# Bias product in pairs of 64 stationary columns, and the channels of a bank in runs of 32 and 96

## Chip, cores and metric

One Trainium2 chip, one core. The metric is the device time of one execution in microseconds (us); lower is better. Single instructions are given in nanoseconds (ns).

## What is computed

The input `x` is `(8, 32, 32, 384)`: 8 images of 32x32 pixels with 384 channels, in fp32. After a group norm (32 groups) the result is `x` plus the sum of two branches:

```python
def _L0_conv_ref(x, w1, b1, w2, b2, bias_w, bias_b):        # x is the normed input
    bias = x @ bias_w.T + bias_b                            # 384 x 384, every pixel
    xb = x.reshape(B, H, W, 4, 96)                          # 4 blocks of 96 channels
    xf = jnp.fft.rfftn(xb, axes=(1, 2), norm='ortho')
    xr, xi = (xf.real, xf.imag)
    r1 = relu(block_mul(xr, w1[0]) - block_mul(xi, w1[1]) + b1[0])
    i1 = relu(block_mul(xr, w1[1]) + block_mul(xi, w1[0]) + b1[1])
    r2 = block_mul(r1, w2[0]) - block_mul(i1, w2[1]) + b2[0]
    i2 = block_mul(r2, w2[1]) + block_mul(i1, w2[0]) + b2[1]
    out = jnp.fft.irfftn(complex(r2, i2), s=(H, W), axes=(1, 2), norm='ortho')
    return out.reshape(B, H, W, C) + bias
x = x + _L0_conv_ref(_gn(x), ...)
```

## The kernel before

The Fourier transforms are matmuls with tables. The work goes image by image (`image(b, p, ...)` on each engine: L703 for TensorE, L829 for ScalarE, L1007 for VectorE), and the order on each engine is written out by hand, with semaphores between them. The bias product is done on the frequency side: it is added to the second block product in the same PSUM bank, and the inverse transform along the width takes both back together.

The stages of one image on TensorE (`mm` at L520 issues every matmul, so all carry L521 in the profile):

- `c1` (L560): the first block product; units 0 to 7 use 128 stationary columns and 192 moving ones, unit 8 uses 32 stationary columns and 96 moving ones, 48 matmuls over the four quarters of a bank's partitions.
- `p3` (L599), with `p1` (L523) of the next image between: transforms along the height and, of the next image, along the width.
- `p4` (L622): the transform back along the height, 96 stationary columns and 128 moving ones; `c2_bias` of item 0 stands in its middle.
- the second block product with the bias, 8 items `gi` of 128 rows by 384 channels, each in a bank of its own (`g_bank`, L302). `c2_bias` (L657) opens the bank with 3 channel tiles `ct` of 3 matmuls each (`mm3`, L554: values are split into a high and a low fp16 part, and high x high, high x low and low x high are added). Its stationary operand is a strided column set of `y` (every 8th of 1024, two bytes each), 128 columns; 384 moving columns of `biasw`. `c2_rho` (L672) adds the block product: for each of 4 blocks, real and imaginary part and 3 products, two matmuls with 64 stationary columns and 96 moving ones, one into partitions 0 to 63 of the bank and one into 64 to 127: 24 pairs, 48 matmuls an item. Item 0 has one more matmul for each pair (`rhoX`), into partitions 64 to 127.
- `p6` (L691): the inverse transform along the width, 3 matmuls of 128 stationary and 384 moving columns for each of 8 tiles, the first three tiles ahead of `c2_rho` of item 7.

The order in the second product is: bias 1 and 2 after `p4`; rho 0, rho 1, `mean` of the next image, rho 2, bias 3, rho 3, `variance` of the next image, bias 4, rho 4, bias 5, rho 5, bias 6, rho 6, bias 7, `p6` tiles 0 to 2, rho 7, `p6` tiles 3 to 7, then `c1` of the next image. The last image has no `mean` and `variance`, and its bias 0 is spread over `p3` in three pieces.

Where the 96 channels of a block lie in a bank is told by `block_columns` (L434). In the order of channels in memory (`order`, L1170) a group of four columns holds three channels of one of blocks 0 to 2 and one channel of block 3. So `c2_rho` writes blocks 0 to 2 as three columns out of every four, and block 3 as every fourth column:

```python
if blk < 3:
    return bank[:, 128 * blk:128 * blk + 128].rearrange("p (i q) -> p i q", q=4)[:, :, 0:3]
return bank[:, 3:CH:4].rearrange("p (q i) -> p i q", q=3)
```

ScalarE and VectorE take each finished bank out as `g` high (L818) and `g` low (L996), 384 columns each. VectorE then adds `x` to the product of `p6` (`add_x`, L999, its instruction is L1004), which SyncE stores. `c1` of the next image waits for the first additions (L573), and `c2_bias` of item `gi` waits for the low part of item `gi - 3` (L667).

The weights are scaled and split once, in the first image: `biasw` by ScalarE (L827, high) and VectorE (`weight_low`, L1105, low, called at L1025), `w2s` by GpSimd (L781 to L784), which `c2_rho` awaits at its first item (L675).

Of the kernel before, what the change touches and what calls it, by code (L numbers as in the profile page):

```python
# [23 lines left out]
BATCHES, SIDE, CH = 8, 32, 384  # L24
# [3 lines left out]
NT = 3  # L28
# [184 lines left out]
def spectral_block_kernel(nc, x, w1, b1, b1h, w2, w2t, b2, bias_wt, bias_b, tab_d, tab16_d, marks_d, out):  # L213
# [7 lines left out]
    with ctx:  # L221
# [212 lines left out]
        def block_columns(bank, blk):  # L434


            if blk < 3:
                return bank[:, 128 * blk:128 * blk + 128].rearrange("p (i q) -> p i q", q=4)[:, :, 0:3]
            return bank[:, 3:CH:4].rearrange("p (q i) -> p i q", q=3)

        def rho_x(s, j, bank):

# [2 lines left out]
            for c in range(2):  # L445
                blk = 2 * (j - 8) + c
                src = bank[0:BC, 132 * c:132 * c + 132]
                for of, at in ((0, 12), (64, 76)):
# [4 lines left out]


        w1_parts = ([w1R[:, s, :, :, :].rearrange("k b a n -> k (b a n)") for s in range(2)], w1raw.rearrange("k b a n -> k (b a n)"), s1[:, :])
        bias_parts = ([biasw[:, s, :, :].rearrange("k b n -> k (b n)") for s in range(2)], biasraw.rearrange("k b n -> k (b n)"), sbias[:, :])
        w2_parts = ([w2s[0:BC + 3, s, :, :, :].rearrange("k b a n -> k (b a n)") for s in range(2)],
                    w2f[0:BC + 3].rearrange("k b a n -> k (b a n)"), w2scale[0:BC + 3, :])

        block = ctx.enter_context(nc.Block())  # L460

# [57 lines left out]
        def _(pe):  # L519
# [137 lines left out]
            def c2_bias(b, p, gi, more, first, cts=range(NT)):  # L657

                if first and gi == 0:
                    pe.wait_ge(bias_ready, 2)  # L660
                if gi < 2 and not more:
                    pass
                elif gi < 3:
                    pe.wait_ge(spec_sum, 9 * b + 7 + gi)
                else:
                    pe.wait_ge(gh_ready, 8 * b + 8 + gi - 2)
                    pe.wait_ge(gl_ready, 8 * b + 8 + gi - 2)  # L667
                for ct in cts:
                    mm3(g_bank(gi, more)[:, 0:CH], [y[p][:, s, ct, :, :].rearrange("k a n -> k (a n)")[:, gi:1024:8] for s in range(2)],
                        [biasw[:, s, ct, :] for s in range(2)], ct == 0, False, skip_group_check=True)  # L670

            def c2_rho(b, gi, more, first):  # L672

# [75 lines left out]
        @block.gpsimd  # L749
        def _(pool):  # L750

            done = [0]

            def do(ins):
                done[0] += 1
                ins.then_inc(pool_prep, 1)
                pool.wait_ge(pool_prep, done[0])

            def all_peak(own, over_all):
                nc.gpsimd.partition_all_reduce(over_all, own, 128, bass.bass_isa.ReduceOp.max).then_inc(peak_reduced, 1)  # L760

            pool.wait_ge(peak_ready, 1)
            all_peak(extreme[:, 0:2], peaks1[:, :])
            pool.wait_ge(peak_reduced, 1)

            pool.wait_ge(w2_in, 16 * N_W2)
            pool.wait_ge(consts_in, 16)
            do(nc.gpsimd.tensor_copy(w2f[0:BC, :, 0, :], w2raw[0:BC, :, 0, :]))
            do(nc.gpsimd.tensor_scalar(w2f[0:BC, :, 1, :], w2raw[0:BC, :, 1, :], -1.0, None, ALU.mult))
            do(nc.gpsimd.tensor_scalar(w2f[BC:BC + 3, :, 0, :], w2raw[BC:BC + 3, :, 0, :], rowscale[BC:BC + 3, :], None, ALU.mult))  # L770
            pool.wait_ge(second_largest, 2)
            do(nc.gpsimd.tensor_copy(extreme[BC:BC + 3, 4:5], extreme[BC:BC + 3, 2:3]))
            do(nc.gpsimd.memset(extreme[BC:BC + 3, 2:3], 0.0))
            pool.wait_ge(s1_ready, 1)
            do(nc.gpsimd.tensor_tensor(extreme[:, 2:5], extreme[:, 2:5], coef[:, 2:5], ALU.mult))
            do(nc.gpsimd.tensor_scalar(extreme[:, 3:5], extreme[:, 3:5], s1[:, :], None, ALU.mult))
            all_peak(extreme[:, 2:5], peaks2[:, :])
            pool.wait_ge(peak_reduced, 2)
            pool.wait_ge(s2_ready, 1)

            (high, rest), src, scale = w2_parts  # L781
            do(nc.gpsimd.tensor_scalar(src, src, scale, None, ALU.mult))
            do(nc.gpsimd.tensor_copy(high, src))
            nc.gpsimd.tensor_tensor(rest, src, high, ALU.subtract).then_inc(w2_ready, 1)  # L784

# [108 lines left out]
        def _(dve):  # L894
# [104 lines left out]
            def add_x(b, p, t):  # L999

                dve.wait_ge(o_prod, 8 * b + t + 1)
                if t % 4 == 0:
                    dve.wait_ge(stored[t // 4], 16 * b + 16)
                nc.vector.scalar_tensor_tensor(out=o_sb[:, t, :], in0=o_bank[t % 4][:, 0:CH], scalar=unscale[:, :], in1=x_sb[p][:, t, :],  # L1004
                                               op0=ALU.mult, op1=ALU.add).then_inc(o_ready, 1)

            def image(b, p, more=True, first=False):  # L1007
# [13 lines left out]
                for u in range(1, 9):  # L1021
                    spectrum_sum(b, u)
                    r_low(b, u - 1)
                    if first and u == 3:
                        weight_low(*bias_parts, bias_ready)  # L1025
                r_low(b, 8)

                for j in range(10):
# [76 lines left out]
            def weight_low(dst, src, scale, ready):  # L1105

                dve.wait_ge(ready, 1)
                low(dst[1], src, scale, dst[0]).then_inc(ready, 1)

            def second_forms():  # L1110

# [83 lines left out]
```

## Time and profile before

| | |
|---|---|
| median of 3 runs | 493.6 us (493.12 to 493.98) |
| the profiled execution | 493.3 us, its span 491.4 us |
| granted TensorE clock, mean | 0.982 |
| TensorE busy with matmuls | 462.8 us, 94% |
| TensorE weight loads | 402.8 us, 82% |
| VectorE, ScalarE, GpSimd busy | 327.0, 238.1, 15.3 us |
| chain that ended last | TensorE 87%, VectorE 5%, issue 3%, ScalarE 3% |

Busy time of TensorE is the union of its matmuls, each counted from its start to its modelled end, some 0.2 us or more; so a group of matmuls is best measured from its own start to the start of the group behind it. In a timeline one line stands for several instructions: its start, the time from the first start to the last end, and how many there are.

### The profile page before, as it was taken

The page shows a single profiled execution, that of the slowest core. Times are in us where ns is not written, and L with a number is a line of the kernel's source. Part 1 is how long each engine was busy: PE and PEld are TensorE (multiplying, and loading weights), DVE is VectorE, ACT ScalarE, POOL GpSimd, SP SyncE. Part 2 cuts the span into 40 slices and gives each one's busy share as a digit, 9 for nine tenths or more (in the row PEclk, how much of TensorE's full clock was granted, in tenths as well). Part 3 has the DMA queues.
Part 4 walks back from the last instruction along what each step waited for, and adds up shares of the span by engine and source line. Part 5 has one row for each costly group of instructions (what it writes and reads, how often), then busy time and mean ns, then how long its engine had stood idle before and what let it go on. Part 6 is the DMA issues. An engine that isn't in the chain of part 4 may idle for free.

```text
span 491.4 us, 15722 instructions
## 1 busy us (share of the span) xinstructions
PE 462.8 (94%) x6728; PEld 402.8 (82%) x6728; DVE 327.0 (67%) x769; ACT 238.1 (48%) x567; POOL 15.3 (3%) x16
## 2 busy tenths in 40 slices
PE   5476899999999999999999999999999999999996
PEld 5374688799888898799988998889987998887884
DVE  3695975578566884668756784668756785668524
ACT  3733483257542674247632683337732575425510
POOL 0030700000000000000000000000000000000000
PEclk9679999999999999999999999999999999999999
DMA  7640000250005100070003300070002500030003
GB/s 219 172 148 2 1 1 13 81 201 1 3 35 191 69 1 3 33 259 1 3 23 134 137 1 3 35 256 3 3 13 87 193 3 2 35 129 3 1 3 129
DMA packets 11637, 32.37 MB, mean 66 GB/s; under 512 B 4196, under 2 KB 5904, under 8 KB 11568
## 3 DMA queue, kind: packets, MB, share of 16 engines
q1 hardware_dynamic: 11568, 31.36, 18.1%
q8 instruction: 54, 0.88, 0.7%
q14 instruction: 15, 0.12, 0.1%
HBM read 15.63 MB, written 12.58 MB: 57 GB/s over the span
## 4 chain that ended last, share of the span: by engine, by line
PE 87%; DVE 5%; issue 3%; ACT 3%; DMA 1%; POOL 0%; DVEq 0%; SPq 0%; POOLq 0%; ACTq 0%
PE bank L521 87%; DVE r L989 1%; DVE rsum L982 1%; DMA x_sb<-in_x 1%; ACT y L813 1%; ACT junk L801 1%; DVE o_sb L1004 0%; DVE z L914 0%; ACT rho L848 0%; DVE extreme L1124 0%; ACT r L823 0%; DVE biasw L914 0%; ACT junk L804 0%; ACT z L833 0%; DVE rho L914 0%
## 5 line engine op out<-in xcount | busy, mean ns | idle before, releaser
L521 PE MATMUL bank<-w2s,rho 96*64 96x96 f16 (+1 forms) x3072 | 119.9, 247 | 0.0
L521 PEld LDWEIGHTS bank<-w2s,rho 96*64 96x64 f16 (+1 forms) x3072 | 107.9, 125 | 11.4 <-issue 11.3
L521 PE MATMUL bank<-biasw,y 128*128 128x384 f16 x576 | 105.4, 330 | 0.1
L521 PEld LDWEIGHTS bank<-biasw,y 128*128 128x128 f16 x576 | 78.6, 146 | 14.0 <-issue 0.2
L818 ACT ACTIVATE g<-bank 128x384 f16<-128x384 f32 x64 | 31.1, 485 | 98.3 <-PE bank L521 98.3
L996 DVE SCALAR_TENSOR_TENSOR g<-g,bank 128x384 f16<-128x384 f16 x64 | 35.4, 553 | 56.9 <-ACT g L818 56.9
L521 PE MATMUL bank<-w1R,y 128*128 128x192 f16 (+3 forms) x768 | 59.5, 228 | 4.4 <-ACT y L813 3.2
L833 ACT ACTIVATE z<-bank 128x384 f16<-128x384 f32 x72 | 35.3, 490 | 56.0 <-PE bank L521 56.0
L521 PEld LDWEIGHTS bank<-tab,x_sb 128*128 128x128 f32 x384 | 51.1, 201 | 9.1 <-issue 6.0
L521 PE MATMUL bank<-tab,x_sb 128*128 128x128 f32 x384 | 52.7, 285 | 6.0 <-DMA x_sb<-in_x 5.8
L914 DVE SCALAR_TENSOR_TENSOR z<-bank,z 128x384 f16<-128x384 f32 x72 | 39.7, 557 | 25.7 <-ACT z L833 24.7
L521 PE MATMUL bank<-w1I,y 128*128 128x192 f16 (+1 forms) x384 | 53.4, 249 | 0.0
L914 DVE SCALAR_TENSOR_TENSOR rho<-bank,rho 96x64 f16<-96x64 f32 (+1 forms) x128 | 49.9, 428 | 5.1 <-PE bank L521 3.5
L521 PEld LDWEIGHTS bank<-tab,r 128*96 128x96 f16 (+1 forms) x864 | 50.8, 123 | 3.0 <-ACT r L823 1.0
L521 PE MATMUL bank<-tab,r 128*96 128x128 f16 (+2 forms) x864 | 51.6, 219 | 1.2 <-ACT r L823 0.7
L823 ACT ACTIVATE r<-rsum 128x384 f16<-128x384 f32 (+1 forms) x72 | 37.3, 519 | 28.7 <-DVE rsum L982 28.3
L521 PE MATMUL bank<-z,tab 128*128 128x384 f16 (+1 forms) x216 | 45.1, 330 | 6.3 <-DVE rsum L982 6.2
L989 DVE SCALAR_TENSOR_TENSOR r<-rsum,r 128x384 f16<-128x384 f32 (+1 forms) x72 | 45.9, 638 | 5.1 <-ACT r L823 3.2
L521 PEld LDWEIGHTS bank<-w1R,y 128*128 128x128 f16 (+3 forms) x768 | 38.4, 98 | 7.8 <-ACT y L813 3.4
L982 DVE SCALAR_TENSOR_TENSOR rsum<-bank,b1s 128x384 f32<-128x384 f32 (+1 forms) x72 | 39.0, 552 | 5.0 <-PE bank L521 4.8
L1004 DVE SCALAR_TENSOR_TENSOR o_sb<-bank,unscale,x_sb 128x384 f32<-128x384 f32 x64 | 35.0, 610 | 7.6 <-PE bank L521 7.6
L914 DVE SCALAR_TENSOR_TENSOR y<-yraw,rstd,y 128x1024 f16<-128x1024 f32 x24 | 30.9, 1292 | 10.9 <-ACT y L813 10.9
(103 smaller groups left out, 421.5 us busy)
## 6 DMA issues: line engine op xcount, KB each, us to landing
x_sb<-in_x SPq DMA_DIRECT2D x16, 768.0 KB, 6.5
out<-o_sb SPq DMA_DIRECT2D x14, 768.0 KB, 4.1
y<-y SPq DMA_DIRECT2D x24, 128.0 KB, 2.7
out<-o_sb SPq DMA_DIRECT2D x8, 192.0 KB, 1.9
tab<-in_tab SPq DMA_DIRECT2D x1, 642.0 KB, 4.7
o_sb<-in_bias_wt SPq DMA_DIRECT2D x4, 144.0 KB, 2.7
b1s<-in_b1h SPq DMA_DIRECT2D x1, 384.0 KB, 5.2
o_sb<-in_w SPq DMA_DIRECT2D x2, 144.0 KB
```

Source lines behind the costliest of these rows:

```text
L521: return nc.tensor.matmul(o, lhsT, rhs, start=start, stop=stop, **kw)
L801: nc.scalar.activation(junk[:, 0:768].rearrange("k (a m) -> k a m", m=384), full_units(ct), ACT.Square, accum_out=sumsq[:, 0, ct:ct + 1]). ...
L813: nc.scalar.activation(y[p][:, 0, ct, :, :], yraw[:, ct, :, :], ACT.Copy, scale=rstd[:, ct:ct + 1]).then_inc(yh_ready, 1)
L818: nc.scalar.activation(g[:, 0, gi, :], g_bank(gi, more)[:, 0:CH], ACT.Copy, scale=G_EVAC).then_inc(gh_ready, 1)
L823: nc.scalar.activation(r[0:rows, 0, u, :], rsum[0:rows, u, :], ACT.Relu).then_inc(rh_ready, 1)
L833: nc.scalar.activation(z[:, 0, u, :], b_bank[u % 3][:, 0:CH], ACT.Copy, scale=Z_EVAC).then_inc(zh_ready, 1)
L914: return nc.vector.scalar_tensor_tensor(out=out, in0=value, scalar=factor, in1=high, op0=ALU.mult, op1=ALU.subtract)
L982: nc.vector.scalar_tensor_tensor(out=rsum[0:rows, u, :], in0=c_bank[u % 3][0:rows, 0:CH], scalar=H_EVAC, in1=b1s[0:rows, u // 4, :], op0=A ...
L989: nc.vector.scalar_tensor_tensor(out=r[0:rows, 1, u, :], in0=rsum[0:rows, u, :], scalar=0.0, in1=r[0:rows, 0, u, :], op0=ALU.max, op1=ALU. ...
L996: nc.vector.scalar_tensor_tensor(out=g[:, 1, gi, :], in0=g[:, 0, gi, :], scalar=-1 / G_EVAC, in1=g_bank(gi, more)[:, 0:CH], op0=ALU.mult, ...
L1004: nc.vector.scalar_tensor_tensor(out=o_sb[:, t, :], in0=o_bank[t % 4][:, 0:CH], scalar=unscale[:, :], in1=x_sb[p][:, t, :], op0=ALU.mult, ...
```

## The change

Four things are changed, and all follow from one: the columns of a bank are in another order. (The constants of the kernel and the order of channels in memory stay.)

- `block_columns`: the bank is now four parts of 96 columns, one for each place `q` in a group of four. Block `blk` of 0 to 2 has 32 columns side by side in each of the first three parts, block 3 has the fourth part whole.
- `biasw` and `w2s` are stored with their columns in the matching order: GpSimd and ScalarE read or write permuted when they split them, and VectorE does the low part of `biasw` in three instructions, one for each channel tile, in place of one.
- `c2_bias` issues each of its nine products as two matmuls with 64 stationary columns, one for each half of the bank's partitions, in place of one with 128.
- `add_x` reads the bank permuted, so that its output has the order in memory.

```diff
-            if blk < 3:
-                return bank[:, 128 * blk:128 * blk + 128].rearrange("p (i q) -> p i q", q=4)[:, :, 0:3]
-            return bank[:, 3:CH:4].rearrange("p (q i) -> p i q", q=3)
+            if blk < 3:
+                return bank[:, 0:3 * BC].rearrange("p (q c i) -> p q c i", q=3, c=3)[:, :, blk, :]
+            return bank[:, 3 * BC:CH]
...
-        bias_parts = ([biasw[:, s, :, :].rearrange("k b n -> k (b n)") for s in range(2)], biasraw.rearrange("k b n -> k (b n)"), sbias[:, :])
-        w2_parts = ([w2s[0:BC + 3, s, :, :, :].rearrange("k b a n -> k (b a n)") for s in range(2)],
-                    w2f[0:BC + 3].rearrange("k b a n -> k (b a n)"), w2scale[0:BC + 3, :])
+        bias_parts = ([biasw[:, s, :, :].rearrange("k b (q p) -> k b q p", q=4) for s in range(2)], biasraw.rearrange("k b (p q) -> k b q p", q=4), sbias[:, :])
+        w2_parts = ([w2s[0:BC + 3, s, :, :, :].rearrange("k b a (q i) -> k (b a) i q", q=3) for s in range(2)],
+                    w2f[0:BC + 3].rearrange("k b a (i q) -> k (b a) i q", q=3))
...
             def c2_bias(b, p, gi, more, first, cts=range(NT)):
 
                 if first and gi == 0:
-                    pe.wait_ge(bias_ready, 2)
+                    pe.wait_ge(bias_ready, 1 + NT)
...
+                bank = g_bank(gi, more)
                 for ct in cts:
-                    mm3(g_bank(gi, more)[:, 0:CH], [y[p][:, s, ct, :, :].rearrange("k a n -> k (a n)")[:, gi:1024:8] for s in range(2)],
-                        [biasw[:, s, ct, :] for s in range(2)], ct == 0, False, skip_group_check=True)
+                    for of, w in ((0, 0), (0, 1), (1, 0)):
+                        for part in range(2):
+                            mm(bank[64 * part:64 * part + 64, 0:CH], y[p][:, of, ct, part, gi:512:8], biasw[:, w, ct, :],
+                               ct == 0 and of == 0 and w == 0, False, skip_group_check=True)
...
-            (high, rest), src, scale = w2_parts
-            do(nc.gpsimd.tensor_scalar(src, src, scale, None, ALU.mult))
+            (high, rest), src = w2_parts
+            whole = w2f[0:BC + 3].rearrange("k b a n -> k (b a n)")
+            do(nc.gpsimd.tensor_scalar(whole, whole, w2scale[0:BC + 3, :], None, ALU.mult))
             do(nc.gpsimd.tensor_copy(high, src))
             nc.gpsimd.tensor_tensor(rest, src, high, ALU.subtract).then_inc(w2_ready, 1)
...
-                nc.vector.scalar_tensor_tensor(out=o_sb[:, t, :], in0=o_bank[t % 4][:, 0:CH], scalar=unscale[:, :], in1=x_sb[p][:, t, :],
+                nc.vector.scalar_tensor_tensor(out=o_sb[:, t, :].rearrange("k (p q) -> k p q", q=4),
+                                               in0=o_bank[t % 4][:, 0:CH].rearrange("k (q p) -> k p q", q=4), scalar=unscale[:, :],
+                                               in1=x_sb[p][:, t, :].rearrange("k (p q) -> k p q", q=4),
                                                op0=ALU.mult, op1=ALU.add).then_inc(o_ready, 1)
...
-                        weight_low(*bias_parts, bias_ready)
+                        bias_low(*bias_parts, bias_ready)
...
+            def bias_low(dst, src, scale, ready):
+
+                dve.wait_ge(ready, 1)
+                for ct in range(NT):
+                    low(dst[1][:, ct], src[:, ct], scale, dst[0][:, ct]).then_inc(ready, 1)
```

## Rows read from the trace of the kernel before

**Rows 1.** The page: span, and busy time of each engine.
```profile
span 491.4 us, 15722 instructions
PE 462.8 (94%) x6728; PEld 402.8 (82%) x6728; DVE 327.0 (67%) x769; ACT 238.1 (48%) x567; POOL 15.3 (3%) x16
```

**Rows 2.** Busy time by window: second product of image 4; columns in its heading.
```profile
core 0: us, PE busy (x) PEld busy (x) DVE busy (x) ACT busy (x) POOL busy (x), PEclk, DMA share, GB/s
235.30:265.80 30.50, 30.50 (x507) 25.24 (x504) 18.19 (x55) 12.73 (x38) 0.00 (x0) 1.00 0.05 16
```

**Rows 3.** Timeline of TensorE in that stage (start, length, group).
```profile
243.56 1.71 PE L521 MATMUL bank<-w2s,rho 99*64 99x96 f16 x48
245.21 1.69 PE L521 MATMUL bank<-biasw,y 128*128 128x384 f16 x9
246.82 1.71 PE L521 MATMUL bank<-w2s,rho 99*64 99x96 f16 x48
...
248.93 1.64 PE L521 MATMUL bank<-biasw,y 128*128 128x384 f16 x9
250.50 1.71 PE L521 MATMUL bank<-w2s,rho 99*64 99x96 f16 x48
...
258.66 1.69 PE L521 MATMUL bank<-biasw,y 128*128 128x384 f16 x9
260.18 1.63 PE L521 MATMUL bank<-g,tab 128*128 128x384 f16 x9
...
265.85 0.41 PE L521 MATMUL bank<-w1R,y 128*128 128x192 f16 x3
```

**Rows 4.** Timeline of TensorE in rho 0: starts of rhoX matmuls, every third matmul.
```profile
238.93 0.23 PE L521 MATMUL bank<-w2s,rhoX 96*64 96x96 f16 x1
...
240.06 0.23 PE L521 MATMUL bank<-w2s,rhoX 96*64 96x96 f16 x1
...
240.54 0.29 PE L521 MATMUL bank<-w2s,rhoX 99*64 99x96 f16 x1
...
241.04 0.29 PE L521 MATMUL bank<-w2s,rhoX 96*64 96x96 f16 x1
```

**Rows 5.** Timeline of TensorE: unit 8 of `c1`, and the group behind it.
```profile
217.38 0.72 PE L521 MATMUL bank<-w1R,y 128*32 128x96 f16 x48
218.03 1.15 PE L521 MATMUL bank<-z,tab 128*128 128x384 f16 x6
```

**Rows 6.** Timeline of TensorE: bias 0 in the middle of `p4`.
```profile
230.47 1.63 PE L521 MATMUL bank<-biasw,y 128*128 128x384 f16 x9
231.94 3.55 PE L521 MATMUL bank<-tab,r 128*96 128x128 f16 x60
```

**Rows 7.** Groups of weight loads by form: busy us, mean ns of one, idle before.
```profile
L521 PEld LDWEIGHTS bank<-w2s,rho 96*64 96x64 f16 x2048 | 96.2, 128 | 0.0
L521 PEld LDWEIGHTS bank<-biasw,y 128*128 128x128 f16 x576 | 78.6, 146 | 14.0 <-issue 0.2
...
L521 PEld LDWEIGHTS bank<-tab,r 128*96 128x96 f16 x672 | 43.6, 123 | 3.0 <-ACT r L823 1.0 <-ACT rho L848 0.6
...
L521 PEld LDWEIGHTS bank<-w1R,y 128*32 128x32 f16 x288 | 3.5, 96 | 1.3 <-issue 1.3
```

**Rows 8.** Timeline of weight loads: the first pair of rho 3.
```profile
246.82 0.11 PEld L521 LDWEIGHTS bank<-w2s,rho 99*64 99x64 f16 x2 [0.27 <-issue]
```

**Rows 9.** Timeline of VectorE: the last five additions of `x`.
```profile
264.56 2.71 DVE L1004 SCALAR_TENSOR_TENSOR o_sb<-bank,unscale,x_sb 128x384 f32<-128x384 f32 x5
```

**Rows 10.** Groups of ScalarE by form: contiguous read of a bank, and permuted one.
```profile
L833 ACT ACTIVATE z<-bank 128x384 f16<-128x384 f32 x72 | 35.3, 490 | 56.0 <-PE bank L521 56.0
...
L793 ACT ACTIVATE yraw<-bank 128x512 f32<-128x512 f32 x48 | 28.5, 593 | 14.7 <-PE bank L521 14.7
```

**Rows 11.** Timeline of VectorE in the first image.
```profile
48.88 3.38 DVE L989 SCALAR_TENSOR_TENSOR r<-rsum,r 128x384 f16<-128x384 f32 x1
52.19 1.41 DVE L914 SCALAR_TENSOR_TENSOR biasw<-o_sb,sbias,biasw 128x1152 f16<-128x1152 f32 x1
```

**Rows 12.** Timeline of GpSimd in the first image.
```profile
52.79 2.12 POOL L783 CAST w2s<-g 99x1536 f16<-99x1536 f32 x1
55.00 3.29 POOL L784 TENSOR_TENSOR w2s<-g,w2s 99x1536 f16<-99x1536 f32 x1
```

## Prediction, made before the changed kernel was run

> **What bounds the kernel now.** I read the page first: in a span of 491.4 us TensorE has matmuls in flight for 462.8 us, and no other engine is above 67% [rows 1]. Then the busy time by window: in the second product of one image, 30.5 us long, TensorE is never without a matmul, while VectorE works 18.2 us and ScalarE 12.7 us of it, at the full granted clock [rows 2]. So this stage lasts as long as TensorE's own stream, and what is taken from the stream is taken from the time, eight times over. The question is what the stream's pace is made of, and "busy" cannot tell; starts can.
>
> **The pace of the pairs.** In the timeline an item of rho (24 pairs) takes 1.65 us to the start of the bias group behind it [rows 3]. Item 0 lets me see the two kinds of block apart, since its extra matmuls stand alone in the timeline: from 238.93 to 240.06 are ten triples, 0.113 us each, in blocks 0 to 2; from 240.54 to 241.04 are three, 0.167 us each, in block 3 [rows 4]. In a triple two of three matmuls go to partitions 64 to 127, so one matmul costs that half of the bank 0.0565 us in blocks 0 to 2 and 0.0833 us in block 3. Both stream 96 columns; they differ in where they write: three columns of four, against every fourth. If the bank is written in aligned couples of columns, the first touches 64 couples and the second 96; two equations give 0.83 ns a couple and 3.3 ns beside it. A whole item then is 18 x 0.0565 + 6 x 0.0833 = 1.52 us, and the 0.13 us that is left of 1.65 belongs to the passage to the bias group.
>
> Unit 8 of `c1` shows matmuls of 96 columns that write side by side: 48 of them in 0.65 us, passage included [rows 5]; in four quarters at once that is 12 in a row, at most 54 ns each, and with a passage of 0.13 to 0.16 us taken off, 41 to 43 ns.
>
> **Part 1, the runs of 32 and 96.** After the change every rho matmul writes 48 couples: 48 x 0.83 + 3.3 = 43.3 ns a pair, an estimate from the fit above. Bounds: 40.8 ns (unit 8's pace) and 56.5 ns (nothing gained in blocks 0 to 2, if something else than writing sets their pace). I take 43.3, since unit 8 is the nearest row and agrees. In an image the upper half of the partitions takes 7 x 24 + 48 = 216 matmuls, 162 in blocks 0 to 2 and 54 in block 3: 162 x 0.0565 + 54 x 0.0833 = 13.65 us now, 216 x 0.0433 = 9.35 us then. **Minus 4.30 us an image.** The page "PSUM — Partial Sum Buffer" of the Trainium skill (Specifications) has the bank in lines of 8 bytes and says that an access that isn't contiguous slows matmuls; that is the couple above, and the fit is this case's number for it.
>
> **Part 2, the passages.** Bias inside `p4`, where nothing changes between full and halved array, takes 1.47 us for nine [rows 6]. Between two rho items it takes 1.61 us (245.21 to 246.82), left towards rho only, 1.57 us (248.93 to 250.50), entered from rho only, 1.52 us (258.66 to 260.18) [rows 3]. So coming from halves costs 0.13 (end of rho) + 0.05 us, going to halves 0.10 us. With bias in halves too: bias 3, 5 and 6 stand between rho items and lose both, 3 x 0.27 = -0.81 us (with 0.13 + 0.14 of the two starts); bias 7 loses 0.18 and leaves to `p6` with 0.10, -0.08; bias 4 behind the variance and bias 1, 2 behind `p4` only move a passage from their end to their start, 0; bias 0 in the middle of `p4` gets two new ones, +0.20. Together **-0.69 us**. The three passages from rho to mean, variance and `p6` stay.
>
> **Part 3, bias in pairs.** Nine matmuls at 162.5 ns become nine pairs. Two halves run side by side in rho; with the 3.3 ns beside 384/2.4 = 160 ns a pair is 163.3 ns, **+0.06 us an image** for 72 pairs. Lower end 0; upper end is that the two don't overlap, see the rivals. Loads: 18 of 64 columns in place of 9 of 128, with a step of 16 bytes. Loads of 32, 96 and (strided) 128 columns take 96, 123 and 146 ns [rows 7], so 64 more columns cost 27 ns and even the strided load of 128 costs some 60 ns above its fixed part; two such in a row, 120 ns, still fit under a pair of 163 ns. The cover is the stream itself.
>
> The rule that speaks against this is in the Trainium skill: "TensorEngine Tiling (Array Packing)", Restrictions and Gotchas, says that column tiling excludes the fast weight load, and "TensorE: Matmul & The Clock Gate", LDWEIGHTS, puts a load at its columns divided by 1.2 ns. By that, 64 columns take 53 ns and a rho pair could not go below it. The trace disagrees with the figure: a load of 96 columns in `p4` would need 80 ns by it, and the 27 ns for 64 more columns [rows 7] are half of it.
>
> **Part 4, VectorE and the rest.** `add_x` reads its bank with a step of 96 columns in runs of four. No row has VectorE do that; ScalarE's permuted read of 512 columns takes 593 ns against 490 ns for 384 contiguous ones [rows 10], 0.8 ns for each further column, so order costs it nothing. I take 0. The place where it would count: the fifth addition starts at 264.56 + 0.53 and ends near 265.70, and `c1` of the next image, which waits for it, starts at 265.85 [rows 3, 9]. Both run from rho 7's end, so the margin of 0.15 us stays. Doubled reading (0.4 us more for each of two) would cost 0.65 us an image, 4.5 us in all: the upper end.
> First image: the low part of `biasw` is one instruction of 1.41 us [rows 11] and becomes three at the spacing of 0.53 us of 384 columns [rows 9], +0.17. GpSimd's cast and subtraction, 2.12 and 3.29 us [rows 12], get a permuted side. Their result is needed only at rho 0 and isn't late for it, but VectorE is held up while GpSimd works: 384 columns take it 3.38 us there and about 0.6 us elsewhere [rows 9, 11]. TensorE waits for VectorE in that stretch. Ends: 0 and +5.4 (both double); I take +0.3, near the row of ScalarE, whose permuted side is free.
>
> **The sum.** -4.30 - 0.69 + 0.06 = -4.93 us an image; the last image has one more such bias (no variance ahead of bias 4) and six passages about its pieces of bias 0, partly in waits, about even. 8 x 4.93 = 39.4; less 0.5 in the first image: -38.9 us. The profiled execution took 493.3 us, 0.3 below the median: 493.3 - 38.9 = 454.4, so **454.5 us** against the median.
>
> **What is late next.** The stage shrinks from 30.5 to about 25.6 us; VectorE's 18.2 us in it [rows 2] become 71%, so it is still not the bound, but its waits get shorter.
>
> **Rivals.**
> 1. *Something is late next* (10%): the capture of a bank, the scales and the low part of the next `y` share VectorE and ScalarE, and one chain that has 12 us of idle now [rows 2] doesn't fit in 5 us less. If a fifth of the gain stays in a wait, 1 us an image: 462 us. For it: a shorter stage; against: 7 us remain idle.
> 2. *Loads set the pace of blocks 0 to 2* (10%): two loads of 64 columns one after the other at 2.4 columns a ns are 53.3 ns, plus 3.3 is 56.7, the very pace seen. Then 216 x (0.0565 - 0.0433) = 2.85 us an image stay: 477 us. Against: the first pair's two loads end together within 0.11 us [rows 8], so they run side by side; a triple has three loads and still costs only the two writes of its half [rows 4]; unit 8 loads 128 columns in 41 to 43 ns [rows 5]. The skill's load rule would give the same time, by 53 ns a load.
> 3. *Slower: the halves of a bias pair don't run side by side* (5%). Both stream the same 384 columns of `biasw` at once; rho pairs stream different ones, so no row shows this. Then each of 576 pairs takes 325 ns: +94 us, 548 us. It decides from 38.9 / 576 = 68 ns more, a pair of 230 ns.
> 4. *The order of writing isn't it* (2%): block 3 is slow for another reason, only passages are saved: 8 x 0.63 = 5 us, 488 us.
>
> **Numbers.** The forecast has 73%. The range holds it with its bounds (40.8 ns a pair gives 450; one of the unknowns at its upper end gives 459 to 460) and rival 1: 448 to 467, some 83%. A measurement of this kernel tells about 0.2% (1 us) from no change. Faster: 73 + 10 + 10 + 2 = 95, of which I leave one for the same: 94%; same 1%; slower 5%.
>
> **What would show it.** In the changed timeline: triples of item 0 at 0.087 us in all four blocks (0.113 in rival 2); rho items at 1.04 us to a bias start; nine bias pairs, 18 matmuls, in 1.47 us (2.9 in rival 3), 1.57 with one passage; the stage 25.6 us without idle TensorE (rival 1: waits on VectorE or ScalarE within it); L1004 still 610 ns. A rho item above 1.3 us or bias above 1.7 us would make the forecast wrong.

## The result, and the profile after

The changed kernel takes 469.91 us (median of 4 runs, 468.5 to 470.83) against 493.79 us: a ratio of 0.9513, interval 0.9497 to 0.9528. It is 5% faster, and 15 us slower than forecast. The profiled execution took 468.5 us. Its page, the head and the chain that ended last, against [rows 1]:

```profile
span 466.7 us, 16876 instructions
PE 428.3 (92%) x7304; PEld 388.3 (83%) x7304; DVE 336.4 (72%) x771; ACT 239.5 (51%) x567; POOL 24.1 (5%) x16
...
PE 85%; DVE 7%; issue 3%; ACT 2%; DMA 1%; POOL 0%; DVEq 0%; SPq 0%; POOLq 0%; ACTq 0%
```

TensorE's busy time fell by 34.5 us and the span by only 24.7. GpSimd, which does nothing after the first image, has 24.1 us in place of 15.3. That is the first sign that the missing time is not in the stage that repeats.

The second product of image 4, by window and in the timeline of TensorE (start, length, group), against [rows 2] and [rows 3]:

```profile
core 0: us, PE busy (x) PEld busy (x) DVE busy (x) ACT busy (x) POOL busy (x), PEclk, DMA share, GB/s
233.82:259.42 25.60, 25.60 (x569) 23.08 (x568) 18.01 (x55) 12.61 (x37) 0.00 (x0) 1.00 0.06 19
```

```profile
228.63 1.74 PE L522 MATMUL bank<-biasw,y 128*64 128x384 f16 x18
230.30 3.58 PE L522 MATMUL bank<-tab,r 128*96 128x128 f16 x60
...
241.63 1.70 PE L522 MATMUL bank<-biasw,y 128*64 128x384 f16 x18
243.17 1.20 PE L522 MATMUL bank<-w2s,rho 99*64 99x96 f16 x48
...
246.41 1.20 PE L522 MATMUL bank<-w2s,rho 99*64 99x96 f16 x48
247.45 1.70 PE L522 MATMUL bank<-biasw,y 128*64 128x384 f16 x18
248.99 1.20 PE L522 MATMUL bank<-w2s,rho 99*64 99x96 f16 x48
```

A rho item now takes 1.04 us to the start of the bias group behind it (246.41 to 247.45; 1.65 before). The stage is 25.60 us long in place of 30.50, with TensorE never idle. A bias group between rho items takes 1.54 us (247.45 to 248.99), not the 1.47 forecast, and bias 0 in the middle of `p4` takes 1.67 us against 1.47 in [rows 6].

In item 0 the extra matmuls again stand alone. Triples are 0.0857 us apart from one end to the other, in all four blocks (twelve triples from 236.94 to 237.97, six from 238.31 to 238.82), where [rows 4] had 0.113 and 0.167:

```profile
236.94 0.20 PE L522 MATMUL bank<-w2s,rhoX 99*64 99x96 f16 x1
...
237.97 0.20 PE L522 MATMUL bank<-w2s,rhoX 99*64 99x96 f16 x1
...
238.31 0.21 PE L522 MATMUL bank<-w2s,rhoX 96*64 96x96 f16 x1
...
238.82 0.21 PE L522 MATMUL bank<-w2s,rhoX 96*64 96x96 f16 x1
```

Now the first image. GpSimd's last three instructions and VectorE's in the same stretch, against [rows 12] and [rows 11]:

```profile
48.64 4.16 POOL L787 TENSOR_SCALAR g<-g,w2scale 99x1536 f32<-99x1536 f32 x1 [6.96 <-issue]
52.88 7.14 POOL L788 CAST w2s<-g 99x1536 f16<-99x1536 f32 x1
60.10 7.54 POOL L789 TENSOR_TENSOR w2s<-g,w2s 99x1536 f16<-99x1536 f32 x1
```

```profile
49.05 3.29 DVE L994 SCALAR_TENSOR_TENSOR r<-rsum,r 128x384 f16<-128x384 f32 x1
52.27 8.51 DVE L919 SCALAR_TENSOR_TENSOR biasw<-o_sb,sbias,biasw 128x384 f16<-128x384 f32 x3
60.70 0.55 DVE L987 SCALAR_TENSOR_TENSOR rsum<-bank,b1s 128x384 f32<-128x384 f32 x1
61.16 6.36 DVE L994 SCALAR_TENSOR_TENSOR r<-rsum,r 96x384 f16<-96x384 f32 x1
```

The cast takes 7.14 us (2.12 before), the subtraction 7.54 (3.29). While each runs, VectorE stands in one instruction that ends within 0.2 us of it: the second of the three low parts takes 6.88 us, where the first and third take 0.9 each, and the next `r` takes 6.36. TensorE waits for VectorE's sums (idle ahead, and releaser, at the end of a line):

```profile
61.30 1.20 PE L522 MATMUL bank<-z,tab 128*96 128x384 f16 x3 [7.07 <-DVE rsum L987]
68.05 1.14 PE L522 MATMUL bank<-z,tab 128*128 128x384 f16 x3 [5.56 <-DVE rsum L987]
68.98 3.75 PE L522 MATMUL bank<-tab,r 128*96 128x128 f16 x48
```

The last of these lines, 3.75 us here, took 2.86 us in every later image: in the changed kernel the granted clock was at its lower level, 1.2 GHz, from 57.2 to 70.9 us, a stretch that begins 3 us into the first of these two waits and holds the second. In the kernel before it was at the upper level, 2.4 GHz, in these same microseconds.

**The books of the miss.** The start of rho 0 in each image divides the span into three parts:

| | before | after | measured | forecast |
|---|---|---|---|---|
| start to rho 0 of image 0 | 68.9 | 80.9 | +12.0 | +0.5 |
| from there to rho 0 of image 7 | 392.3 | 360.7 | -31.6 | -39.4 with the row below |
| from there to the end | 30.2 | 25.1 | -5.2 | in the row above |

An image in the steady part takes 51.99 us, before 56.49: 4.50 less, where 4.93 were forecast. So of 14 us too few, 11.5 are in the first image and 2.7 in what follows it. The twelve runs below ask what each is made of.

### The profile page after: what moved, and what is told of

It is laid out like the page before. It is cut to its first block, busy times and chain, and to the rows that moved or that the text cites. A ratio compares the mean times of both kernels' runs of the same rounds, so it can differ in the third digit from the quotient of the medians.

```text
span 466.7 us, 16876 instructions
## 1 busy us (share of the span) xinstructions
PE 428.3 (92%) x7304; PEld 388.3 (83%) x7304; DVE 336.4 (72%) x771; ACT 239.5 (51%) x567; POOL 24.1 (5%) x16
## 4 chain that ended last, share of the span: by engine, by line
PE 85%; DVE 7%; issue 3%; ACT 2%; DMA 1%; POOL 0%; DVEq 0%; SPq 0%; POOLq 0%; ACTq 0%
PE bank L522 85%; DVE biasw L919 2%; DVE r L994 1%; DMA x_sb<-in_x 1%; DVE y L919 1%; ACT junk L806 1%; DVE o_sb L1009 0%; DVE rsum L987 0%; DVE z L919 0%; DVE extreme L1137 0%; ACT junk L809 0%; DVE extreme L1142 0%; ACT y L818 0%; DVE rho L919 0%; DVE b1s L1110 0%
## 5 line engine op out<-in xcount | busy, mean ns | idle before, releaser
L522 PE MATMUL bank<-biasw,y 128*64 128x384 f16 x1152 | 109.4, 335 | 0.0
L522 PEld LDWEIGHTS bank<-biasw,y 128*64 128x64 f16 x1152 | 93.5, 196 | 2.3 <-issue 1.0
L522 PEld LDWEIGHTS bank<-w2s,rho 96*64 96x64 f16 (+1 forms) x3072 | 81.4, 109 | 4.4 <-issue 2.5
L522 PE MATMUL bank<-w2s,rho 96*64 96x96 f16 (+1 forms) x3072 | 84.4, 207 | 0.0
L919 DVE SCALAR_TENSOR_TENSOR z<-bank,z 128x384 f16<-128x384 f32 x72 | 39.7, 557 | 25.7 <-ACT z L838 24.7
L994 DVE SCALAR_TENSOR_TENSOR r<-rsum,r 128x384 f16<-128x384 f32 (+1 forms) x72 | 48.4, 672 | 5.1 <-ACT r L828 3.1
L522 PEld LDWEIGHTS bank<-z,tab 128*128 128x128 f16 (+1 forms) x216 | 21.5, 106 | 26.5 <-DVE rsum L987 18.3
```

Of the source, the lines that this page charges most:

```text
L522: return nc.tensor.matmul(o, lhsT, rhs, start=start, stop=stop, **kw)
L919: return nc.vector.scalar_tensor_tensor(out=out, in0=value, scalar=factor, in1=high, op0=ALU.mult, op1=ALU.subtract)
L994: nc.vector.scalar_tensor_tensor(out=r[0:rows, 1, u, :], in0=rsum[0:rows, u, :], scalar=0.0, in1=r[0:rows, 0, u, :], op0=ALU.max, op1=ALU. ...
```

## The experiments

**Which permuted instruction costs the first image its time.** The first kernel takes GpSimd's permutation out of the changed kernel, the second puts it alone into the kernel before.

```diff
-        w2_parts = ([w2s[0:BC + 3, s, :, :, :].rearrange("k b a (q i) -> k (b a) i q", q=3) for s in range(2)],
-                    w2f[0:BC + 3].rearrange("k b a (i q) -> k (b a) i q", q=3))
+        w2_parts = ([w2s[0:BC + 3, s, :, :, :].rearrange("k b a n -> k (b a n)") for s in range(2)],
+                    w2f[0:BC + 3].rearrange("k b a n -> k (b a n)"))
```

> The changed kernel, with the second weights split on GpSimd in their natural order again (so the block product uses them with their columns out of place; everything else as changed). Theory: GpSimd's permuted cast and subtraction (7.14 and 7.54 us against 2.12 and 3.29) hold VectorE up and cost the first image about 12 us; without them the cast and the subtraction are back at 2.1 and 3.3 us, rho 0 of image 0 starts near 69 us, and the time is 457 to 459 us. Rival: the first image lost its time by the permuted instructions of ScalarE and VectorE for the bias weights (2.36 us against 1.25, and three low parts in 8.5 us); then the time stays above 465 us.

> The kernel before, with nothing changed but GpSimd's split, which writes and reads the second weights permuted (so the block product uses them out of place). Theory: GpSimd costs 9.3 us more, VectorE is held up for most of that, and the time is 9 to 12 us above the kernel before, near 504 us. Rival (bias weights are the cause): no more than 3 us above.

Measured: 462.42 us (ratio 0.9368 to the kernel before, interval 0.9346 to 0.939), and 502.62 us (1.0169, 1.0154 to 1.0184). Neither theory had it whole. GpSimd's permutation is worth 7.5 us in the one and 8.5 in the other, so it is the larger part; but 4 to 5 us of the first image stay. The trace of the first shows where: GpSimd is back at 1.58 and 3.44 us, and the three low parts of `biasw` still take

```profile
53.07 6.32 DVE L919 SCALAR_TENSOR_TENSOR biasw<-o_sb,sbias,biasw 128x384 f16<-128x384 f32 x3
```

In the kernel before this was one instruction. It started at 52.19, ahead of GpSimd's cast at 52.79, and took 1.41 us although the cast began during it [rows 11, 12]. As three, the second and third meet GpSimd at work (1.97 and 3.59 us; the first took 0.91). The second kernel has the one instruction and the slow GpSimd, and there the `r` behind it are held instead:

```profile
52.50 1.41 DVE L915 SCALAR_TENSOR_TENSOR biasw<-o_sb,sbias,biasw 128x1152 f16<-128x1152 f32 x1
53.83 0.54 DVE L983 SCALAR_TENSOR_TENSOR rsum<-bank,b1s 128x384 f32<-128x384 f32 x1
54.30 6.26 DVE L990 SCALAR_TENSOR_TENSOR r<-rsum,r 96x384 f16<-96x384 f32 x1
60.48 0.54 DVE L983 SCALAR_TENSOR_TENSOR rsum<-bank,b1s 128x384 f32<-128x384 f32 x1
60.95 6.87 DVE L990 SCALAR_TENSOR_TENSOR r<-rsum,r 128x384 f16<-128x384 f32 x1
```

`rsum`, which reads one of its inputs from a bank, takes 0.54 us beside the same GpSimd instruction; `r`, with both in SBUF, lasts to about its end. The Trainium skill states this in "SBUF — State Buffer", Who interferes with whom: a VectorE instruction with two SBUF inputs and a GpSimd instruction that reads SBUF exclude each other, and the later one waits for the whole of the other. The rows shown here agree with that, and the other way round too: where a low part has 0.8 us still to run when the contiguous cast begins, the cast takes 2.12 us [rows 11, 12]; where it has 0.3, as in the first kernel here, 1.58.

**What the two other parts of the change are worth.** Bias in pairs alone, put into the kernel before; and the changed kernel with bias in one matmul again.

```diff
-                    mm3(g_bank(gi, more)[:, 0:CH], [y[p][:, s, ct, :, :].rearrange("k a n -> k (a n)")[:, gi:1024:8] for s in range(2)],
-                        [biasw[:, s, ct, :] for s in range(2)], ct == 0, False, skip_group_check=True)
+                    for of, w in ((0, 0), (0, 1), (1, 0)):
+                        for part in range(2):
+                            mm(bank[64 * part:64 * part + 64, 0:CH], y[p][:, of, ct, part, gi:512:8], biasw[:, w, ct, :],
+                               ct == 0 and of == 0 and w == 0, False, skip_group_check=True)
```

The second kernel makes the same edit backwards in the changed kernel.

> The kernel before, with only the bias product in pairs of 64 stationary columns; the order of channels in a bank, the weights and the additions stay. Theory by the starts of the changed kernel: between rho items a bias group costs 1.535 us in place of 1.61 and the end of rho before it 0.13 us less, so bias 3, 5, 6 save 0.2 us each, bias 4 and 7 about nothing, bias 0 within p4 costs 0.42 with what it moves, 1 and 2 nothing: 0 to 0.4 us an image less, 490.5 to 494 us in all. Rival (the forecast's term for the passages, 0.69 us an image): 488 us.

> The changed kernel with its bias product in one matmul of 128 stationary columns again. Theory: the rho pairs take 43.3 ns in all blocks and give 4.3 us an image, 34 us, the first image loses 12: 470 to 473 us, 0 to 3 us above the changed kernel. Rival (the passages are worth 0.69 us an image): 475.5 us.

Measured: 490.52 us (0.9925, interval 0.9906 to 0.9944), and 471.22 us (0.9531, 0.9517 to 0.9545). Both theories hold; the forecast's gain of 0.63 us an image by pairs and passages does not come out. By the periods of an image, which repeat to 0.01 us:

| | period, us | against the kernel before |
|---|---|---|
| before | 56.49 | |
| pairs only | 56.14 | -0.35 |
| runs only | 52.10 | -4.39 |
| both (the change) | 51.99 | -4.50 |

The runs of 32 and 96 are the change; they give 4.39 us an image, where the forecast had 4.30. Pairs on top of them give 0.11 us, where it had 0.63. With strided writes, a pair group between rho items costs 1.48 + 1.52 us with the rho item before it (timeline of the first kernel), against 1.65 + 1.61 in [rows 3]:

```profile
250.92 1.69 PE L521 MATMUL bank<-w2s,rho 99*64 99x96 f16 x48
252.40 1.69 PE L521 MATMUL bank<-biasw,y 128*64 128x384 f16 x18
253.92 1.69 PE L521 MATMUL bank<-w2s,rho 99*64 99x96 f16 x48
```

That is 0.26 us saved, the forecast's 0.27. With runs it is 1.15 + 1.61 us for one matmul each (timeline of the second kernel)

```profile
250.69 1.22 PE L522 MATMUL bank<-w2s,rho 99*64 99x96 f16 x48
251.84 1.68 PE L522 MATMUL bank<-biasw,y 128*128 128x384 f16 x9
253.45 1.22 PE L522 MATMUL bank<-w2s,rho 99*64 99x96 f16 x48
```

against 1.04 + 1.54 for pairs: 0.18 us, and 0.20 at some items. And bias 0 in the middle of `p4` costs more than its two passages: `p4` with it takes 7.97 us (225.84 to 233.81) where it took 7.55.

**Is it the write, and what does the moving operand cost.** The forecast put the pace of the strided pairs down to where they write. This kernel keeps the runs in the bank, and reads the weights with a step instead.

```diff
-                                      w2s[0:rows, w, blk, 2 * part + ri, :], False, ...
+                                      w2s[0:rows, w, blk, 2 * part + ri, :].rearrange("k (i q) -> k q i", q=3), False, ...
```

(so also for the extra matmuls of item 0, with `w2_parts` flat as in the first experiment and block 3 written as `"p (q i) -> p q i"`)

> The changed kernel, but the second weights keep their natural order in memory (GpSimd splits them as before) and the block product's matmuls read them as moving operand with a step of three elements, so that the output is the reference's again. Theory: the write into the bank, not the read of the moving operand, set the pace of the rho pairs; then the pairs stay at 43.3 ns, the period of an image at 52.0 us, and the time is that of e1_w2_flat, 461 to 464 us. Rival: a moving operand with a step is slower as well; a rho item then goes above 1.04 us, at twice the time per column +1.0 us an item, and the total to 470 us or more.

Measured: 502.18 us (1.016, interval 1.014 to 1.018). The theory fell: the rival is right, and by more than it said. A rho item takes 1.60 us (timeline)

```profile
258.19 1.77 PE L522 MATMUL bank<-w2s,rho 99*64 99x96 f16 x48
259.79 1.68 PE L522 MATMUL bank<-biasw,y 128*64 128x384 f16 x18
```

some 67 ns a pair, with every write in runs. So there are two limits: the way out, 57 and 83 ns a pair for three columns of four and for every fourth, and the way in, with a step of 6 bytes. That doesn't take back the first, since in the kernel before the moving operand had no step; it shows that the permutation could not have been moved into the matmul for nothing.

**GpSimd's short runs.** The changed kernel with the loops of GpSimd's views turned round.

```diff
-        ... .rearrange("k b a (q i) -> k (b a) i q", q=3) ...  .rearrange("k b a (i q) -> k (b a) i q", q=3)
+        ... .rearrange("k b a (q i) -> k (b a) q i", q=3) ...  .rearrange("k b a (i q) -> k (b a) q i", q=3)
```

> The changed kernel, with GpSimd's permuted cast and subtraction written so that the innermost loop has 32 elements (weights read with a step of three, written side by side) in place of 3. Theory: GpSimd pays for each short innermost run; then the cast is near 2.1 us again and the subtraction near 3.4, and the time 461 to 464 us. Rival: any step costs it the same; cast and subtraction stay at 7 us each and the time at 470 us.

Measured: 462.92 us (0.9367, interval 0.9349 to 0.9385), as the theory had it. The same elements are moved between the same places; the innermost run is 32 and not 3:

```profile
54.67 2.56 POOL L788 CAST w2s<-g 99x1536 f16<-99x1536 f32 x1
57.32 3.85 POOL L789 TENSOR_TENSOR w2s<-g,w2s 99x1536 f16<-99x1536 f32 x1
```

2.56 and 3.85 us against 7.14 and 7.54. An edit of a few letters is worth 7 us. With the loops the step changes sides, though: the changed kernel reads the weights side by side and writes them 64 bytes apart (32 fp16 columns), this one reads them 12 bytes apart and writes side by side. No run has short runs without the wide step, so which of the two GpSimd pays for stays open; what is shown is the worth of this order of loops.

**Without GpSimd's split.** ScalarE makes the high part, VectorE the low part in three instructions, one for each `q` (the views of `w2s` are those of the kernel just above).

```diff
+                    if first and m == 3:
+                        (w2_high, _), w2_src = w2_parts
+                        nc.scalar.activation(w2_high, w2_src, ACT.Copy, scale=w2scale[0:BC + 3, :]).then_inc(w2_ready, 1)
...
+                    if first and u == 6:
+                        (w2_high, w2_low), w2_src = w2_parts
+                        dve.wait_ge(w2_ready, 1)
+                        for q in range(3):
+                            low(w2_low[:, :, q, :], w2_src[:, :, q, :], w2scale[0:BC + 3, :], w2_high[:, :, q, :]).then_inc(w2_ready, 1)
...
-            do(nc.gpsimd.tensor_scalar(whole, whole, w2scale[0:BC + 3, :], None, ALU.mult))
-            do(nc.gpsimd.tensor_copy(high, src))
-            nc.gpsimd.tensor_tensor(rest, src, high, ALU.subtract).then_inc(w2_ready, 1)
```

> The changed kernel, with the second weights scaled and split by ScalarE (high part, in its idle time) and VectorE (low part, three instructions), as the first weights are; GpSimd's three instructions are gone. Theory: VectorE was held up whenever an instruction of it with both inputs in SBUF met GpSimd at work, about 6 us in the kernel before and 15 us in the changed one; without GpSimd all of that goes, 1.8 us come for the three low parts, and rho 0 of image 0 starts at 65 to 67 us: 454 to 457 us. Rival: the low parts and ScalarE's permuted read take its place; then 462 us as in e1_w2_flat.

Measured: 459.80 us (0.9301, interval 0.9277 to 0.9324). Between the two: the holds are gone, but rho 0 starts only at 72.5 us. VectorE waits 1.97 us for `r` from ScalarE, which is at its permuted read, and its own low parts, ahead of sums that TensorE awaits, take 2.58 us:

```profile
51.84 2.54 DVE L913 SCALAR_TENSOR_TENSOR biasw<-o_sb,sbias,biasw 128x384 f16<-128x384 f32 x3 [1.54 <-ACT biasw L823]
...
58.69 0.56 DVE L988 SCALAR_TENSOR_TENSOR r<-rsum,r 128x384 f16<-128x384 f32 x1 [1.97 <-ACT r L819]
59.16 2.58 DVE L913 SCALAR_TENSOR_TENSOR w2s<-g,w2scale,w2s 99x512 f16<-99x512 f32 x3
```

The first line shows one more cost: with no GpSimd instruction beside them, the three permuted low parts of `biasw` still take 2.54 us, where the one contiguous instruction takes 1.41 [rows 11]. So part of their cost is their own and not GpSimd's.

**Why a bias group costs 1.54 us.** Nine pairs at 163.3 ns are 1.47. This kernel takes the stationary columns side by side.

```diff
-                            mm(..., y[p][:, of, ct, part, gi:512:8], biasw[:, w, ct, :],
+                            mm(..., y[p][:, of, ct, part, 64 * gi:64 * gi + 64], biasw[:, w, ct, :],
```

> The changed kernel, with the stationary columns of the bias pairs taken side by side (64 columns from 64 gi) in place of every eighth, so the bias is that of other pixels; only the address pattern of the weight load changes. Theory: the first pair of a bias group takes 0.24 to 0.28 us in place of 0.16, since a load of 64 columns with a step takes 196 ns (109 without) and the second pair's load isn't covered; then a group between rho items goes from 1.535 to 1.47 us, the period of an image from 51.99 to 51.3 to 51.5 us and the time to 464 to 467 us. Rival: the delay belongs to the passage whatever the load is; 469 to 471 us.

Measured: 466.25 us (0.9435, interval 0.9417 to 0.9452), period 51.44 us (51.88 once), as the theory had it. The group takes 1.46 us (timeline of this kernel), and the loads tell why: the second fence is this kernel's group of weight loads (busy us, mean ns of one), the third that of the changed kernel.

```profile
247.22 1.63 PE L522 MATMUL bank<-biasw,y 128*64 128x384 f16 x18
248.68 1.20 PE L522 MATMUL bank<-w2s,rho 99*64 99x96 f16 x48
```

```profile
L522 PEld LDWEIGHTS bank<-biasw,y 128*64 128x64 f16 x1152 | 62.6, 110 | 23.6 <-issue 1.0
```

```profile
L522 PEld LDWEIGHTS bank<-biasw,y 128*64 128x64 f16 x1152 | 93.5, 196 | 2.3 <-issue 1.0
```

A load of 64 columns with a step of 16 bytes takes 196 ns, without one 110. Where pairs start 163 ns apart it is hidden, but the second pair of a group between rho items starts 237 ns after the first, and 167 here, so each group pays once: 0.07 us between rho items, about 0.09 where the array was whole before it.

This period is 0.66 us under that of runs only (52.10). The forecast had 0.63 for passages and pairs together. So nearly all that the changed kernel lacks of it is the load with a step, though bias 0 within `p4` still costs 0.34 us here, more than the 0.20 of the forecast, and other items make up for it.

**Pairs only where they pay.** From the starts: items 3, 5 and 6 stand between two rho items, all others touch a stage that uses the whole array.

```diff
+                if gi not in (3, 5, 6):
+                    for ct in cts:
+                        mm3(bank[:, 0:CH], [y[p][:, s, ct, :, :].rearrange("k a n -> k (a n)")[:, gi:1024:8] for s in range(2)],
+                            [biasw[:, s, ct, :] for s in range(2)], ct == 0, False, skip_group_check=True)
+                    return
```

> The changed kernel, with the bias product in pairs only where it stands between two rho items (items 3, 5 and 6); items 0, 1, 2, 4 and 7 use one matmul of 128 stationary columns as before. Theory, by the starts of the changed kernel and of e4_runs_only: between rho items a pair group with the end of rho before it takes 1.574 us against 1.751 (3 x 0.177 gained over e4), in the middle of p4, behind p4, behind the variance and ahead of p6 pairs cost 0.33, 0.1, 0.075 and 0.017 us more than one matmul; so the period of an image is 52.10 - 0.53 = 51.57 us against 51.99, and the time 466 to 467.5 us. Rival (passages cost the same everywhere): no difference from the changed kernel, 470 us.

Measured: 468.04 us (0.9475, interval 0.9459 to 0.9491). The period is 51.49 us, 0.50 under the changed kernel's, a little more than expected; the total moved by less, 1.9 us. In the profiled execution rho 0 of image 0 began at 82.6 us and not 80.9, and the delay was there ahead of every bias product: GpSimd's scaling of `w2` began at 50.5 us, against 48.6 in the changed kernel. In the profiled executions of this case that start lies anywhere between 48.6 and 50.5 us, so up to 2 us of a first image are not an edit's. Behind rho 0 of image 7 it took 25.8 us, against 25.1, for a reason that stays open. The rival is out by the period.

**No permuted instruction at all.** The columns of the weights are put in the bank's order where the arguments are laid out, as `x` is. The views of `biasw` and `w2s`, and the one low part of `biasw`, are those of the kernel before.

```diff
+    runs = np.arange(96).reshape(32, 3).T.ravel()
+    cols = order.reshape(96, 4).T.ravel()
...
-        "w2": w2, ... "b2": b2,
-        "bias_wt": np.ascontiguousarray(np.asarray(L0_conv_bias_w).T[:, order]), "bias_b": np.asarray(L0_conv_bias_b),
+        "w2": np.ascontiguousarray(w2[..., runs]), ... "b2": b2, "b2q": np.ascontiguousarray(b2[..., runs]),
+        "bias_wt": np.ascontiguousarray(np.asarray(L0_conv_bias_w).T[:, cols]), "bias_b": ...reshape(4, 96)[:, runs].ravel()),
```

> The changed kernel, with the columns of the second weights, their bias and the bias weights put into the order of the bank where the arguments are laid out for the launch (as the order of x already is), so that no instruction on the chip permutes a weight: GpSimd's split, ScalarE's high part and VectorE's one low part of the bias weights are those of the kernel before. Theory: the whole loss of the first image comes from permuted weight instructions; rho 0 of image 0 starts at about 69 us as before, 12 us earlier than in the changed kernel, and the time is 457 to 459.5 us. Rival: VectorE's share is small and the time stays at e6_pool_long_runs' 462.9 us.

Measured: 457.57 us (0.9254, interval 0.9235 to 0.9273), 12.3 us under the changed kernel, as the theory had it. GpSimd and VectorE are back at their times of before:

```profile
54.04 2.12 POOL L788 CAST w2s<-g 99x1536 f16<-99x1536 f32 x1
56.24 3.29 POOL L789 TENSOR_TENSOR w2s<-g,w2s 99x1536 f16<-99x1536 f32 x1
```

```profile
53.43 1.41 DVE L919 SCALAR_TENSOR_TENSOR biasw<-o_sb,sbias,biasw 128x1152 f16<-128x1152 f32 x1
54.76 0.55 DVE L987 SCALAR_TENSOR_TENSOR rsum<-bank,b1s 128x384 f32<-128x384 f32 x1
55.23 1.34 DVE L994 SCALAR_TENSOR_TENSOR r<-rsum,r 96x384 f16<-96x384 f32 x1
56.49 0.54 DVE L987 SCALAR_TENSOR_TENSOR rsum<-bank,b1s 128x384 f32<-128x384 f32 x1
56.96 2.99 DVE L994 SCALAR_TENSOR_TENSOR r<-rsum,r 128x384 f16<-128x384 f32 x1
```

This closes the first image: 7.5 us by GpSimd's permutation, and 4.9 (462.42 to 457.57, by the medians; rho 0 starts 3.0 us earlier in the profiled executions) by the permuted, three-part split of `biasw`. No run tells the order of its columns from its being three instructions.

**Together.** The last two kernels add the pairs of 3, 5, 6, and then also take the split of `w2s` away from GpSimd, contiguous now, ScalarE behind `r` 3 (`m == 2`) and VectorE in one instruction at `u == 5`.

> e12_host_order and e10_pairs_356 together. Theory: the two gains lie in different stretches and add up: 3.4 us below e12_host_order, 454 to 456.5 us. Rival: the first image hides part of it.

> e14_host_356, and the second weights scaled and split by ScalarE (high) and VectorE (low) in place of GpSimd's three instructions. Theory: about 6 us in which VectorE is held up while GpSimd works (3.4, 1.3 and 3.0 us for operations of 0.55) go, a low part of 1536 columns (1.7 us) comes: 3 to 5 us below e14_host_356, 450 to 453 us. Rival: TensorE waits for the low part and the clock is at its lower level in that stretch, as in e7_no_gpsimd_tail; then within 2 us of e14_host_356.

Measured: 455.32 us (0.9218, interval 0.9202 to 0.9233), and 452.89 us (0.9162, 0.9141 to 0.9182). The first gain adds up in the periods (51.49, against 51.99; 3.4 us from rho 0 of image 0 to rho 0 of image 7, as expected), but only 2.3 us are left of it by the medians, and behind rho 0 of image 7 it again takes 25.8 us in place of 25.1; the second is 2.4 us, short of the 3 to 5 expected: rho 0 starts at 67.1 us in place of 70.0. VectorE's low part is not held and holds nothing:

```profile
53.51 0.56 DVE L986 SCALAR_TENSOR_TENSOR rsum<-bank,b1s 128x384 f32<-128x384 f32 x1 [0.29 <-PE bank L522]
54.20 0.56 DVE L993 SCALAR_TENSOR_TENSOR r<-rsum,r 128x384 f16<-128x384 f32 x1
54.67 1.81 DVE L918 SCALAR_TENSOR_TENSOR w2s<-g,w2scale,w2s 99x1536 f16<-99x1536 f32 x1
```

This kernel is the best of the study, 8.4% under the kernel before and 3.6% under the changed one.

## Why the prediction failed, step by step

- **What bounds the kernel, and the pace of the pairs: right.** Two equations over the triples of item 0 gave 0.83 ns for an aligned couple of columns and 3.3 ns beside it. The forecast pair of 43.3 ns (48 x 0.83 + 3.3 is 43.1; unrounded the fit gives 43.3) makes 1.04 us an item, and 1.04 us was measured, with triples alike in all blocks. Part 1 had -4.30 us an image; runs alone gave -4.39. That the loads set the pace (rival 2) is out: 64-column loads are the same, and the pairs are at 43 ns. The third point doesn't prove the couples, though: 48 couples at 0.83 ns take as long as 96 columns at the 0.42 ns of the bias matmuls (384 in 162.5), so a pair in runs may as well be bound by its columns as by its writes.
- **Part 4 is the step that failed**, in its GpSimd term: "I take +0.3, near the row of ScalarE, whose permuted side is free", with +5.4 as the upper end. The first image lost 12.0 us where 0.5 was forecast. The cast and the subtraction grew by 9.3 us, beyond the doubling, in views with innermost runs of three elements, and VectorE and then TensorE stood behind them; with the loops turned round 7.0 us came back. ScalarE reading a bank was no near row for GpSimd, and not even for ScalarE reading SBUF: its high part of `biasw` went from 1.25 to 2.36 us. The holding of VectorE was seen and its price passed over: it is not a share of GpSimd's time, but all of what remains when the instruction arrives.
- **Part 4, the low part of `biasw`: mis-sized.** +0.17 us was the count of three spacings of 0.53. What it cost, with ScalarE's part, is 4.9 us by the medians. The three permuted instructions take 2.54 us by themselves in place of 1.41, and the one instruction of before had slipped in ahead of the cast, where the second of the three could not.
- **Part 3: the pairs do run side by side** (163 ns a pair; rival 3 is out), **but the load was mis-sized.** Some 60 ns above its fixed part was taken from a load of 128 columns; 64 take 196 ns. The cover holds for eight pairs of nine; for the first it isn't there, and the forecast didn't ask what covers the first. This is the second failed term: without the step the period falls by 0.55 us more.
- **Part 2: right as a sum, without that load.** -0.69 and +0.06 us an image were forecast, -0.66 was measured against runs only once the load had no step, and -0.11 with it. Its parts came out less well: a passage between rho items is worth 0.26 with strided writes, as forecast (0.27), and 0.18 to 0.20 with runs, where the end of rho gives 0.12 us in place of 0.16 and the bias group 0.08 in place of 0.10. Bias 0 was put at +0.20 and cost about 0.33 of its own, the rest of the 0.42 being the passage that moved from the end of bias 1 and 2 to the end of `p4`.
- **Part 4, `add_x`: right.** 610 ns before, 610 ns after, with a step of 96 columns in the bank.
- **Rival 1 was wrong in its place.** Nothing is late in the stage that repeats; VectorE is the bound in the first image alone.
- The signs and the largest term were right, and the range of 448 to 467 missed 469.9 by the first image. None of the four rivals is about that image, and neither is any sign of being wrong that the forecast named: a rho item above 1.3 us or a bias group above 1.7 us, and none of the two came.

## What to carry to other kernels

Before a layout is changed for the sake of the loop, price the one-time preparation as its own kernel: find which engine it stands on, what it holds up, and whether the layout can be made where the arguments are laid out. Write GpSimd's views with the long run innermost and, as here, the step on the side that reads (the two were not told apart); and give a doubled instruction count a look at which neighbour it now meets. For matmuls, keep the output in whole runs and the moving operand without a step; divide the array in halves only where the stages on both sides are halved too.

## What was not expected of the hardware

- The order in which a matmul writes its bank sets its pace: pairs of 96 fp32 columns go at 43.3 ns in runs of 32 and 96, at 56.7 with three columns of four, at 83.3 with every fourth. About 0.83 ns for an aligned couple of columns (48, 64 and 96 of them) fits all three.
- A moving operand with a step of 6 bytes takes 67 ns a pair, against 43.3 without, although both write the same runs.
- A load of 64 stationary columns takes 110 ns, with a step of 16 bytes 196 ns.
- GpSimd's cast of 1536 columns takes 1.58 us contiguous (2.12 where a VectorE instruction with both inputs in SBUF is in its way), 2.56 when it reads with a step of three elements in runs of 32, 7.14 to 7.68 when it writes 64 bytes apart in runs of three.
- ScalarE's and VectorE's reads of a bank cost nothing more when permuted. Reads of SBUF do: 1152 columns with a step of 16 bytes take ScalarE 2.36 us in place of 1.25, and VectorE 2.54 us as three instructions of 384 in place of 1.41 as one without a step.
